# New tables of places for a batched attention and conditional-convolution kernel, with small work moved from VectorE to GpSimd

## The reference, cut to what matters

```python
xn = group_norm(x, gn_w, gn_b)                       # 32 groups of 8 channels
q, k, v = split(einsum('oc,bchw->bohw', qkv_w, xn) + qkv_b)
attn = softmax(einsum('bhdm,bhdn->bhmn', q, k) / 8)  # 4 heads of 64, 1024 x 1024
x2 = x + proj(einsum('bhmn,bhdn->bhdm', attn, v))

rw = sigmoid(mean(x2, pixels) @ router_w.T + router_b)   # 8 gates for each image
W_l = einsum('be,eoihw->boihw', rw, w_l)                 # 8 experts mixed, three layers
h = relu(bn(conv1x1(x2, W_1))); h = relu(bn(conv3x3(h, W_2)))
out = relu(bn(conv1x1(h, W_3)) + x2)
```

## Time and profile before

| | |
|---|---|
| median of 3 runs | 2106.51 us (2098.74 to 2114.05) |
| the profiled execution | 2096.82 us, its span 2095.0 us |
| granted TensorE clock, mean | 0.984 |
| PE busy | 1960.1 us, 94% |
| DVE busy | 1440.0 us, 69% |
| POOL busy | 1118.7 us, 53% |
| ACT busy | 1045.7 us, 50% |
| DMA moved | 119.35 MB |

### The profile page before, as it was taken

How to read it: one execution, slowest core, us unless ns; L and a number is a source line. 1 busy time by engine, 2 the same in 40 slices (tenths; PEclk the granted TensorE clock), 3 DMA queues, 4 the chain that set the end, 5 groups by cost and what they waited for, 6 DMA issues and landing times.

```text
span 2095.0 us, 26308 instructions
## 1 busy us (share of the span) xinstructions
PE 1960.1 (94%) x8072; PEld 1061.8 (51%) x8072; DVE 1440.0 (69%) x1638; ACT 1045.7 (50%) x1346; POOL 1118.7 (53%) x533
## 2 busy tenths in 40 slices
PE   4999999999999999999999989999899999999994
PEld 3555555545555455555555545455554555545431
DVE  5658768486784957758586785857858587685743
ACT  3555545454555444555454555454554455554441
POOL 3665555464555545555464564645555555554660
PEclk9999999999999999999999999999999999999997
DMA  3112131121313012130121312113130121301201
GB/s 137 42 26 82 36 101 26 44 74 31 101 31 96 20 36 91 32 105 20 41 81 31 101 30 65 47 36 96 31 101 18 38 87 34 101 24 43 56 27 61
DMA packets 65694, 119.35 MB, mean 57 GB/s; under 512 B 20480, under 2 KB 21248, under 8 KB 65536
## 3 DMA queue, kind: packets, MB, share of 16 engines
q1 hardware_dynamic: 65664, 118.97, 19.4%
HBM read 54.68 MB, written 17.04 MB: 34 GB/s over the span
## 4 chain that ended last, share of the span: by engine, by line
PE 79%; DVE 12%; issue 5%; DMA 2%; ACT 2%; DVEq 0%; SPq 0%; POOL 0%; ACTq 0%
PE PV L590 19%; PE SB L461 12%; PE S L574 11%; PE MS L555 10%; PE S L577 9%; PE SB L498 5%; PE SB L532 4%; DVE mx L763 4%; DVE mix L854 3%; PE SB L492 3%; PE SB L540 3%; DVE rden L841 2%; PE SB L519 1%; DVE o L836 1%; DVE x_lo L755 1%
## 5 line engine op out<-in xcount | busy, mean ns | idle before, releaser
L447 POOL TENSOR_TENSOR psum_p<-psum_p,prob 128x1024 f32<-128x1024 f32 x384 | 931.1, 2425 | 596.4 <-ACT prob L654 589.0
L763 DVE TENSOR_REDUCE mx<-MS 128x1 f32<-128x1024 f32 x500 | 609.9, 1220 | 416.1 <-PE MS L555 413.9
L654 ACT ACTIVATE prob<-S 128x1024 f32<-128x1024 f32 x512 | 523.7, 1024 | 405.1 <-PE S L577 398.6
L590 PE MATMUL PV<-prob,V 128*64 128x512 f32 x2048 | 506.9, 617 | 0.0
L574 PE MATMUL S<-Q,K 128*128 128x512 f32 x1024 | 455.1, 444 | 2.5 <-DVE mx L910 2.5
L577 PE MATMUL S<-Q,K 128*128 128x512 f32 x1024 | 406.1, 397 | 0.3 <-DMA Q<-mrow 0.3
L555 PE MATMUL MS<-K,Q 128*128 128x512 f32 x1000 | 327.8, 409 | 73.3 <-DVE mx L763 73.2
L574 PEld LDWEIGHTS S<-Q,K 128*128 128x128 f32 x1024 | 194.3, 190 | 264.9 <-issue 231.4
L447 POOL TENSOR_TENSOR psum_p<-prob 128x1024 f32<-128x1024 f32 x64 | 151.7, 2370 | 311.3 <-ACT prob L654 311.3
L590 PEld LDWEIGHTS PV<-prob,V 128*64 128x64 f32 x2048 | 125.5, 137 | 266.4 <-issue 240.5
L555 PEld LDWEIGHTS MS<-K,Q 128*128 128x128 f32 x1000 | 176.5, 188 | 162.5 <-DVE mx L763 131.2
(11 more groups left out here) (126 smaller groups left out, 1879.8 us busy)
## 6 DMA issues: line engine op xcount, KB each, us to landing
xin<-in_x_dram SPq DMA_DIRECT2D x16, 1024.0 KB, 8.7
K<-K SPq DMA_DIRECT2D x128, 128.0 KB, 2.2
Q<-Q SPq DMA_DIRECT2D x128, 128.0 KB, 2.3
rz<-z_dram SPq DMA_DIRECT2D x128, 128.0 KB, 2.9
x<-in_x_dram SPq DMA_DIRECT2D x16, 1024.0 KB, 6.2
out_dram<-y SPq DMA_DIRECT2D x64, 256.0 KB, 2.1
V<-v_next SPq DMA_DIRECT2D x16, 512.0 KB, 6.5
hpad<-hpad SPq DMA_DIRECT2D x16, 289.0 KB, 3.1
```

The costliest lines, as they stand in the source:

```text
L447: nc.gpsimd.tensor_tensor(acc, first_in, prob[:, s % PBUF, :, :], ALU.add).then_inc(add_done, 1)
L590: last = nc.tensor.matmul(PV[own(a), :], V[:, b // NH, kt, a * D:a * D + D], prob[:, s % PBUF, a, :], start=(kt == 0), stop=(kt == KT - 1))
L654: nc.scalar.activation(prob[:, s % PBUF, :, :], S[:, s % 2, :, :], ACT.Exp, scale=D ** -0.5).then_inc(exp_done, 1)
L763: nc.vector.reduce_max(mx[:, b % 2, m:m + 1], MS[:, :, :], AX.XY).then_inc(max_read, 1)
```

## The change

The tables of places are new, with one table for PE and ACT (`PLACES`), one for DVE (`WORK`) and one for POOL (`POOL_WORK`). Row maxima run 5 steps ahead, not 4. The experts are no longer all in SBUF: two buffers are refilled by DMA as the mixing goes on, and each is loaded anew for each image. The low part of the input (`x_lo`) and the small numbers of the group norm and the gates (`gdev`, `gvar_in`, `gdev2`, `gvar`, `rden`) are computed on POOL. `pool2` and `poolb` go: the router multiplies `pool4` spread over the columns, in four matmuls for two. The sums `z` go into a bank of `MS`, so that the next fill waits for ACT's copy of them. `conv1`'s result is written by ACT four times, the shifted copy too, with no DMA. The last image's sums are inverted where they are, with no DMA, and its experts are loaded before they are needed.

```diff
-AHEAD = 4
+AHEAD = 5
-MID = {0: [("qk", 0, 5)], 1: [("qk", 0, 7)], 2: [("row", 0, 1)], 3: [("proj", -1, 2)], 4: [("gnb", 1, 0)],
...
+BATCH = 2
+PLACES = {0: [("qk", 0, 6)], 1: [("proj", -1, 0)], 2: [("proj", -1, 1)], 3: [("row", 0, 1)], 4: [("gna", 1, 0), ("proj", -1, 2)],
+          5: [("proj", -1, 3)], 6: [("qk", 0, 7)], 7: [("gnb", 1, 0)], 9: [("router", -1, 0)], 12: [("row", 0, 2)], 13: [("qk", 1, 0)],
+          14: [("qk", 1, 1)], 15: [("v", 1, 0)], 16: [("qk", 1, 2)], 18: [("v", 1, 1)], 19: [("row", 0, 3)], 22: [("qk", 1, 3)],
+          24: [("v", 1, 2)], 25: [("conv3", -1, 0)], 26: [("v", 1, 3)], 27: [("row", 1, 0)], 28: [("conv3", -1, 1)],
+          29: [("conv3", -1, 2), ("conv3", -1, 3)], 30: [("qk", 1, 4)], 31: [("qk", 1, 5)]}
+HALVES = {3: [("z", 0, 0)], 9: [("z", 0, 1), ("conv1", -1, 0)], 10: [("conv2a", -1, 0), ("conv2", -1, 0), ("z", 0, 2)], 15: [("z", 0, 3)]}
...
-RECIPROCAL = {1: (-1, 3), 5: (0, 0), 9: (0, 1), 14: (0, 2)}
-NORMALISE = {2: (-1, 3), 6: (0, 0), 10: (0, 1), 15: (0, 2)}
-STATS_0, STATS_1, NORM, SPLIT, AFFINE_STEP = 1, 2, 6, 7, 10
-MIX_MID = {6: 1}
-MIX_LATE = {5: 1, 6: 1, 7: 1, 8: 1, 9: 1, 10: 2}
+WORK = {1: [("qk", 0, 6), ("proj", -1, 0), ("stats", 1, 0), ("recip", -1, 3)], 2: [("proj", -1, 1), ("stats", 1, 1)],
+        3: [("row", 0, 1), ("norm", -1, 3), ("gna", 1, 0)], 4: [("proj", -1, 2), ("proj", -1, 3)], 8: [("recip", 0, 0), ("gnb", 1, 0)],
+        9: [("router", -1, 0), ("qk", 0, 7), ("mix", -1, 0)], 11: [("mix", -1, 1), ("row", 0, 2)],
+        12: [("norm", 0, 0), ("mix", -1, 2), ("mix", -1, 3)], 14: [("qk", 1, 0), ("mix", -1, 4)], 15: [("mix", -1, 5), ("qk", 1, 1)],
+        16: [("mix", -1, 6)], 17: [("qk", 1, 2)], 18: [("mix", -1, 7), ("row", 0, 3)], 19: [("mix3", -1, 0)], 21: [("recip", 0, 1)],
+        23: [("norm", 0, 1)], 25: [("qk", 1, 3), ("conv3", -1, 0)], 26: [("recip", 0, 2), ("row", 1, 0)],
+        28: [("conv3", -1, 1), ("conv3", -1, 2), ("conv3", -1, 3)], 31: [("qk", 1, 4), ("qk", 1, 5), ("norm", 0, 2)]}
+NORM = {9: 0, 10: 1}
+POOL_WORK = {8: ["deviations"], 10: ["gates", "affine", "split0", "split1"]}
...
-        ex = sb("ex", [P, E, MIX])
+        ex = sb("ex", [P, 2, MIX])
...
+            def load_expert(i, e):
+
+                wait(sp, mix_chain, E * i + e - 1)
+                sp.dma_start(ex[:, e % 2, :], experts[:, e, :]).then_inc(ex_loaded[e % 2], 16)
...
+            def gates(i):
+
+
+                pool.wait_ge(rexp_ready, i + 1)
+                wait(pool, mix_chain, E * i)
+                nc.gpsimd.tensor_tensor(rden[:, :], rexp[:, :], ones[:, 0:E], ALU.add).then_inc(rw_ready, 1)
+
+            def split_x(i, c):
+                pool.wait_ge(xn_ready, 2 * i + c + 1)
+                wait(pool, filled["qk"], 8 * i)
+                nc.gpsimd.tensor_tensor(x_lo[:, c, :], xin[:, c, :], x_hi[:, c, :].bitcast(F32),
+                                        ALU.subtract).then_inc(xsplit_ready, 1)
...
                     pe.wait_ge(add_done, adds_reading(i, KT * f + KT - 1))
+                    pe.wait_ge(max_read, fills)
                     for a in range(2):
-                        last = nc.tensor.matmul(bank[own(a), :], ones[:, 0:D], psum_p[:, f % 2, a, :], start=True, stop=True)
+                        last = nc.tensor.matmul(MS[own(a), 0, :], ones[:, 0:D], psum_p[:, f % 2, a, :], start=True, stop=True)
...
+                wait(pe, read["z"], sums)
...
-                    for hf in range(NH):
-                        at = (1 + hf * rows_hf) * PW + 1
-                        dst = hpad[0:64, at:at + rows_hf * PW].rearrange("p (r w) -> p r w", w=PW)[:, :, 0:W]
+                    for hf, upper in ((0, 0), (1, 0), (0, 1), (1, 1)):
+                        at = (1 + hf * rows_hf) * PW + 1 - upper
+                        dst = hpad[own(upper), at:at + rows_hf * PW].rearrange("p (r w) -> p r w", w=PW)[:, :, 0:W]
...
-                    dve.wait_ge(read["gna"], i + 1)
-                    for c in range(CC):
-                        last = nc.vector.tensor_scalar(gdev[:, c, :], bst[:, c, :, 1], gsum[:, c, 1:2], None, ALU.subtract)
...
-                        nc.vector.tensor_tensor(pool2[:, :], pool4[:, :, 0], pool4[:, :, 1], ALU.add).then_inc(pool_done, 1)
...
-                nc.vector.tensor_scalar(rden[:, :], rexp[:, :], 1.0, None, ALU.add).then_inc(rw_chain, 1)
...
+            def mix_expert(i, e):
+                dve.wait_ge(ex_loaded[e % 2], 16 * (E // 2) * i + 16 * (e // 2) + 16)
...
+                if (kind, f) == ("proj", 0):
+                    reciprocal(B - 1, BLOCKS - 1)
+                    normalise_o(B - 1, BLOCKS - 1)
                 job(kind, B - 1, f, bank)
```

More of the change, by code:

```diff
@@ L77 @@
[L77 to L81, removed]
+BATCH = 2
+TURNS = STEPS // BATCH
+PLACES = {0: [("qk", 0, 6)], 1: [("proj", -1, 0)], 2: [("proj", -1, 1)], 3: [("row", 0, 1)], 4: [("gna", 1, 0), ("proj", -1, 2)],
+          5: [("proj", -1, 3)], 6: [("qk", 0, 7)], 7: [("gnb", 1, 0)], 9: [("router", -1, 0)], 12: [("row", 0, 2)], 13: [("qk", 1, 0)],
[3 rows of a table added]
@@ L268, in jobs_of @@
         def jobs_of(place, t, first, last):
[L269 to L272 removed]
+            return [j for j in place.get(t, []) if in_range(j[1], first, last)]
         def in_range(di, first, last):
@@ L363, in section @@
             def section(i, first, last):
-                load_v1(i)
                 if not last:
                     load_xin(i + 1)
-                for t in range(TURNS):
-                    for kind, di, f in all_jobs(t, first, last):
+                if not first:
+                    move_z(i - 1, BLOCKS - 1)
+                load_v1(i)
+                for n in range(STEPS):
+                    for kind, di, f in jobs_of(PLACES, n, first, last):
                         if kind == "qk":
@@ L447, in section @@
                         nc.gpsimd.tensor_tensor(acc, first_in, prob[:, s % PBUF, :, :], ALU.add).then_inc(add_done, 1)
-                    if s == AFFINE_STEP and not last:
-                        affine(i + 1)
+                    for what in POOL_WORK.get(s, []):
+                        if what == "gates" and not first:
+                            gates(i - 1)
+                        if what == "deviations" and not last:
+                            deviations(i + 1)
+                        if what == "affine" and not last:
+                            affine(i + 1)
+                        if what in ("split0", "split1") and not last:
+                            split_x(i + 1, int(what[5]))
             sections(pool, section)
+            gates(B - 1)
         @block.tensor
@@ L463, in split_mm, with job @@
                 return last
-            def job(kind, i, f, before, bank=SB[:, :], at_end=False):
+            def job(kind, i, f, before, bank=SB[:, :], at_end=False, fills=0):
                 for k, bi, bf in before:
@@ L614, in section @@
             def section(i, first, last):
[L616 to L633, removed]
-                        held = [(kind, i + di, f)]
+                held, sums = ([("row", 0, 0)], 0) if first else ([(LAST[0], i - 1 + LAST[1], LAST[2])], BLOCKS * i)
@@ new lines, in section @@
+                for n in range(STEPS):
+                    at = fill_at(i, n, last)
+                    if at:
+                        max_reduce(*at)
+                    for kind, di, f in jobs_of(WORK, n, first, last):
+                        if kind == "stats":
+                            stats(i + di, f)
+                        elif kind == "recip":
+                            reciprocal(i + di, f)
+                        elif kind == "norm":
+                            normalise_o(i + di, f)
+                        elif kind == "mix":
+                            mix_expert(i + di, f)
+                        elif kind == "mix3":
+                            spread_mix3(i + di)
+                        else:
+                            job(kind, i + di, f)
```

255 lines of the change are left out of this document (143 added, 112 removed).

## The result

| | before | after |
|---|---|---|
| median | 2108.9 us (4 runs) | 2236.07 us (2233.54 to 2238.51, 4 runs) |
| span of the profiled execution | 2095.0 us | 2233.4 us |
| ratio | | 1.0609, 95% interval 1.0566 to 1.0652 |

The account below looks back on a forecast made before the run. PE was taken to bound most of the time, DVE the stretch around the gates. The profiled 2096.8 us, plus 112 (14 x 8), less 12 at the end, gave 2196.8; with 9.7 to the median, 2206 us, range 2165 to 2250.

Parts of the forecast that it names:

- the walk: One section followed job by job with the new tables: waits of 17.9 us against 7.9, so +10.0 for each image.
- The stretch, steps 8 to 19: Part of a section where PE's waits for DVE's reductions and ACT's exp were to sum to 14.9 us.
- T: Zero point of the section's times: the end of z(0,0), after step 7.
- Steps 1 to 4: Low part, proj, statistics and norm before gna: their work was to cost about 2 us.
- the wait for `hpad`: PE's wait for ACT's writing of `hpad`, between conv1 and conv2: 1.5 us, expected to go.
- the count of DVE's own waits: Second count for each image: DVE's work falls 3 us, its waits rise about 6; with other terms, +6.7.
- The end: Last z to norm's end: 9 to 11 us saved; hpad DMA replaced by ACT writes: 1.4; together 12 taken.
- Hidden edits: Experts' DMA, z in `MS`, maxima 5 ahead, SP's waits: expected hidden, save one more pair of maxima before section 0.
- A: Rival: DVE's operations meet POOL as often as on average before, 14 x -3.3, median 2048 us; chance 0.27.
- B: Rival: the alternation costs half of what was walked, +1 for each image, less 12: about 2109 us; chance 0.13.
- C: Rival: 384 KB loads delay small transfers behind them, 4 us an image, 60 more: 2266 us; chance 0.05.
- S: Rival theory tested in the experiments: the stream of experts makes mixes late, 3.3 us for a section; no chance given.

Follow-up runs that it names:

- the spread tables: The changed kernel with the mixing kept out of steps 11 to 15, conv1 and conv2 four steps later and a few jobs moved with them: 2139.17 us, ratio 1.0142.

## Why the prediction was right, step by step

**The direction and the mechanism.** Right: PE waits at fills 14 and 16 for reductions that stand behind norm, mix 2 and mix 3, and behind K's low part and mix 4. Mix 2 and 3 took 6.18 us together, where the walk had 3.4 each, and mix 4 3.02. POOL added without a pause behind the splits, for 14.2 us and not 20. The two runs with short adds show that 8.3 of the 9.8 us hang on POOL's adds.

**The stretch, steps 8 to 19.** The walk lost 14.9 us, of which fill 14 had 4.3, fill 16 4.3, fill 17 2.1. Measured are 3.06, 1.79 and 2.25, and fill 11 0.41 for 1.3; PE waited 0.89 for exp 13 where 1.4 stood, and not for exp 12 where 0.8 stood. With 0.40 at fill 9 and 0.37 at z(0,1) that makes 9.2 us. So more than a third of the walk's waits in this stretch did not come. PE was ready for fill 14 at 20.9 us after T, for fill 16 at 33.3 (the walk: 21.8 and 33.8). The second nearly agrees because of a term that I had not at all: the clock. Over the 30 us from 1320 on the granted clock was 0.89. Behind fill 14's wait qk went at 0.43 us a matmul for 0.23 (from 1323.57 to 1324.85 three stand), and behind fill 17's wait eight matmuls of pv took 3.29 us for 1.94. Counted from these rows, that is about 3 us of PE's own work at the lower of its two levels, 1.2 GHz for 2.4.

**Elsewhere.** Steps 1 to 4 had 2 us in the walk and show 0.7; conv3's reads had 1.0 and show 1.7. The 7.9 us of waits before held 1.5 that never were one. I read the wait for `hpad` from the chain, but PE was at work in it until 1142.24 and began the next job 0.09 us later:

```profile
1141.62 0.62 PE L555 MATMUL MS<-K,Q 128*128 128x512 f32 x2
1142.33 0.39 PE L461 MATMUL SB<-w_hi,x_hi 128*128 128x256 f32 x1
```

So the true base was 6.4, and the walk read against it gives +11.5 us of waits.

**Size.** 14 x 8 = 112 was taken, between 5 and 11 each; 136.8 was measured, 9.8 each. It looks as if the full walk (+10.0) had been exact and the count of DVE's own waits (+6.7) mis-sized. It is the other way round: the waits grew by 7.1 us a section, and 2.7 are PE's longer work. The walk has its number by luck, as waits that are too long stand in it where the clock is missing. The mis-sized term of the forecast is the section: it put the lower clock that follows the waits at nothing. The forecast of 2206 was 30 us short: 25 in these sections, 9 in sections 0 and 15 and 5 in the prologue are missing, and the 9.7 added for the median happened to cover a part, since the changed kernel's profiled execution (2235.56) stood at its median. The whole range, from 2045 to 2250, would have held a faster kernel too; what the run bears out is the forecast of 2165 to 2250 and its mechanism.

**Sections 0 and 15.** Only sections 1 to 14 were counted, as only they have both the splits and the mixing. The other two lost 9.2 us together, nearly one section more.

**The end.** From the last z to the end it takes 38.9 us for 51.2: 12.3 saved, where 12 was taken. From that z (2194.49) to norm's end (2200.27) are 5.8 us for 13.8, so 8.0 saved for the 9 to 11 foretold, since the last image's reciprocal took 3.35 us, above the 3 that I had as its upper bound:

```profile
2196.19 3.35 DVE L906 RECIPROCAL rz<-rz 128x512 f32<-128x512 f32 x1 [1.90 <-ACT rz L769]
2199.58 0.69 DVE L917 TENSOR_TENSOR o<-o,rz 128x512 f32<-128x512 f32 x1
```

Behind norm 4.3 were saved for the 1.4 foretold. The two misses cancel.

**Hidden edits.** The stream was hidden, as said, and shown by the run without it. The prologue, said to cost one more pair and left out of the sum, gave 4.6 us. Of the rivals, A (spread waits, 2048) had its condition, mixes that find POOL idle in step 12, plainly denied; B (half the alternation, 2109) is denied by the time; C (DMA) fell with S.

## What to carry to other kernels

Busy shares hid this loss: DVE and POOL had room, and moving 8 us of open time off DVE looked like a gain. Where two engines exclude each other and both have a queue they take turns, so a mix of 1.0 us took 3.1 and a `rden` of 0.1 took 2.1. Count in each stretch the *number* of such instructions against the queue of the other, and keep them out of steps in which it has one. A table can be tested cheaply by cutting the other engine's work to a few columns with every wait left in place. And when a sum of waits comes out right, compare PE's busy time too: here a quarter of the loss was no wait.

## What the runs showed of the hardware

DVE and POOL, both with work queued, took turns: two mixes of 1.0 us took 6.18 beside adds of 2.4. A DVE instruction with one input waited as well (`rden`, 2104 ns beside POOL's adds of 1024 columns, 103 ns beside adds of 8), and the reductions that read `MS` did not (1217 ns). The chain of waits did not show this wait: it named a DMA of 3.23 us whose removal changed nothing (2235.85 for 2236.07 us). Moving an operation to the engine on which it is shorter did not pay: x_lo on DVE, 1.2 us, came out 1.4% slower than on POOL, 2.4 us (2168.73 for 2139.17 us), with the spread tables and some places a step or two later. PE's waits of 3.06 and 2.25 us were each followed by matmuls at half speed, from 1322.55 to about 1325.3 and from 1338.92 to 1343.1; with short adds, where such waits are gone, the granted clock of the sections was 1.00 for 0.97.
